# The last scans, the last three y and the first tile's index are reordered in a state-space and expert kernel

## What is computed

```python
x = L0_attn_u                              # (16, 512, 256)
xn = layernorm(x)
# state-space part
Bu = einsum('bld,nd->bln', u, B_w)         # u = xn
h[t] = sigmoid(log_lambda) * h[t-1] + Bu[t]    # written in the reference as an FFT convolution
y = einsum('bln,dn->bld', h, C_w) + D * u
# expert part
aff = (xn @ waff.T) / (|xn| * |waff| + 1e-9)
cap = clip(floor(S * sigmoid(aff.mean() - threshold)), 4, S)
mask = one_hot(argmax(softmax(aff))) * (rank of aff within its sequence and expert < cap)
out = sum over experts e of gelu((xn * mask_e) @ W1[e] + b1[e]) @ W2[e] + b2[e]
result = x + y + out
```

## Time and profile before

| | us |
|---|---|
| median of 3 runs (633.16 to 633.51) | 633.2 |
| the profiled execution, its own time | 634.01 |
| its span, first to last instruction | 632.1 |
| outside the span | 1.9 |
| PE busy | 580.8 (92%) |
| DVE, ACT, POOL busy | 431.0, 432.6, 460.8 |
| mean granted TensorE clock | 0.957 |

### The profile page before, as it was taken

How to read it: one execution, slowest core, us unless ns; L and a number is a source line. 1 busy time by engine, 2 the same in 40 slices (tenths; PEclk the granted TensorE clock), 3 DMA queues, 4 the chain that set the end, 5 groups by cost and what they waited for, 6 DMA issues and landing times.

```text
span 632.1 us, 16452 instructions
## 1 busy us (share of the span) xinstructions
PE 580.8 (92%) x4597; PEld 492.8 (78%) x4598; DVE 431.0 (68%) x831; ACT 432.6 (68%) x783; POOL 460.8 (73%) x618
## 2 busy tenths in 40 slices
PE   2987868989889999999999999999999999999992
PEld 1555545657678998989898898989898898989882
DVE  5789998987988989885655555645555555646554
ACT  4877677845978977886766767575766667575750
POOL 1999887971055434888878788888888888888855
PEclk9979778879799999999999999999999999999997
DMA  8993865736321314512222212122212212111110
GB/s 310 412 391 138 267 221 182 239 157 228 111 91 40 101 35 121 182 53 69 70 80 77 77 54 58 52 72 73 68 45 59 75 45 66 57 58 34 52 45 31
DMA packets 33588, 72.63 MB, mean 115 GB/s; under 512 B 6520, under 2 KB 19089, under 8 KB 33553
## 3 DMA queue, kind: packets, MB, share of 16 engines
q1 hardware_dynamic: 21488, 46.67, 20.9%
q0 software_dynamic: 11232, 25.20, 13.1%
q10 hardware_dynamic: 832, 0.31, 0.2%
HBM read 50.64 MB, written 27.00 MB: 123 GB/s over the span
## 4 chain that ended last, share of the span: by engine, by line
PE 75%; DVE 10%; issue 6%; ACT 5%; DMA 2%; POOL 1%; DVEq 0%; ACTq 0%; SPq 0%; POOLq 0%
PE ps_bu L919 10%; PE ps_bu L920 10%; PE ps_bu L921 10%; PE ps_t L890 5%; PE ps_t L892 5%; PE ps_t L891 5%; PE ps_y L892 5%; PE ps_y L890 5%; PE ps_y L891 5%; PE ps_bu L744 3%; ACT area L560 2%; PE ps_t L726 2%; PE ps_y L758 2%; PE ps_num L872 1%; PE ps_t L801 1%
## 5 line engine op out<-in xcount | busy, mean ns | idle before, releaser
L1364 DVE SCALAR_TENSOR_TENSOR ring<-ring,h_scale 128x512 f16<-128x512 f32 x156 | 115.9, 751 | 138.3 <-ACT ring L686 137.5
L919 PE MATMUL ps_bu<-area,ring 128*128 x616 | 167.9, 273 | 0.3 <-issue 0.3
L920 PE MATMUL ps_bu<-area,ring 128*128 x616 | 167.9, 273 | 0.0
L921 PE MATMUL ps_bu<-area,ring 128*128 x616 | 167.9, 273 | 0.0
L686 ACT ACTIVATE ring<-ring,h_act 128x512 f16<-128x512 f32 x144 | 104.0, 722 | 27.1 <-ACT ring L678 27.1
L494 POOL DMA_INDIRECT out<-ring,idx_b x74 | 94.7, 1280 | 17.3 <-issue 12.4
L456 POOL DMA_INDIRECT work<-xn_rows,idx_x x70 | 86.9, 1241 | 24.8 <-issue 24.2
L678 ACT ACTIVATE ring<-ps_t,b1t,inv_in 128x256 f32<-128x256 f32 x156 | 78.6, 556 | 33.2 <-PE ps_t L892 27.9
L504 POOL DMA_INDIRECT work<-base_rows,idx_b x74 | 79.2, 1070 | 17.1 <-issue 15.7
L890 PE MATMUL ps_t<-work,area 128*128 128x256 f16 x312 | 85.1, 273 | 1.7 <-ACT work L588 1.7
L892 PE MATMUL ps_t<-work,area 128*128 128x256 f16 x312 | 85.0, 273 | 0.0
(11 more groups left out here) (289 smaller groups left out, 1074.3 us busy)
## 6 DMA issues: line engine op xcount, KB each, us to landing
ring<-L_ffn_W SPq DMA_DIRECT2D x14, 1024.0 KB, 6.4
xn_rows<-area SPq DMA_DIRECT2D x8, 1024.0 KB, 8.6
base_rows<-area SPq DMA_DIRECT2D x8, 1024.0 KB, 7.2
area<-L_attn_u SPq DMA_DIRECT2D x7, 1024.0 KB, 19.1
work<-L_ffn_W SPq DMA_DIRECT2D x3, 1024.0 KB, 5.8
area<-L_ffn_W SPq DMA_DIRECT2D x3, 1024.0 KB, 5.4
work<-base_rows,idx_b POOLq DMA_INDIRECT x74, 2.8
out<-ring,idx_b POOLq DMA_INDIRECT x74
```

Source lines behind the costliest of these rows:

```text
L919: t.matmul(dst, hh, wh, start=(c == 0), stop=False)
L920: t.matmul(dst, hh, wl, start=False, stop=False)
L921: last = t.matmul(dst, hl, wh, start=False, stop=(c == C - 1))
L1364: v.scalar_tensor_tensor(out=hlo[p][:, cs], in0=h32[:, cs], scalar=h_scale[:, bass.ds(e, 1)], in1=hhi[p][:, cs], op0=ALU.mult, op1=ALU.sub ...
```

## The change

PE forms y of b = 14 before it transposes the last router sums, and y of b = 15 right after the affinity sum, ahead of most of the zero rows. In DVE's loop the denominators move behind `states(15)`. The adds of y for b = 13, 14 and 15 leave DVE: ACT copies `ps_y` to a buffer (`copy_y`), and POOL adds it (`add_y` on POOL, two adds of 128x512 each). The buffers are parts of `g_bc` and `work`, so `base_store(7)` now stands ahead of `raw_in(13)` and `raw_in(14)` in SP's list. ACT's `weight_sum(12)`, which stood ahead of the search, goes into its first half after round n = 5. The places in the second half move from n = 4, 5, 7, 10 to 1, 3, 5, 8. The index is formed in two steps: first the two columns of tile 0 (`idx_ok` 1), then the rest (`idx_ok` 2); POOL gathers tile 0 after the first.

```diff
@@ SP
             base_store(5)
             xn_store(7)
+            base_store(6)
             raw_in(12)
-            base_store(6)
+            base_store(7)
             raw_in(13)
             raw_in(14)
-            base_store(7)
             raw_in(15)
@@ POOL, after the 16 products
+            def add_y(b):
+                pool.wait_ge(s["y_out"], b - MOVED + 1)
+                for q in range(2):
+                    x = slice(q * 2 * D, (q + 1) * 2 * D)
+                    last = g.tensor_tensor(xu_(b)[:, x], y_out[b][:, x], xu_(b)[:, x], ALU.add)
+                last.then_inc(s["base_ok"], 1)
+            pool.wait_ge(s["dx_ok"], 2 * B)
+            add_y(B - 3)
+            add_y(B - 2)
             pool.wait_ge(s["sig_ok"], 1)
...
             g.tensor_scalar(cap, cap, 4.0, float(S), ALU.max, ALU.min).then_inc(s["cap_ok"], 1)
+            add_y(B - 1)
@@ POOL, gathers
+            bound = pool.to_reg(TOKENS - 1)
             pool.wait_ge(s["idx_ok"], 1)
-            bound = pool.to_reg(TOKENS - 1)
...
             for m in range(5):
+                if m == 1:
+                    pool.wait_ge(s["idx_ok"], 2)
                 gates = rows_in(m, m % 4, gates)
@@ ACT
+            def copy_y(b):
+                act.wait_ge(s["y_ok"], b + 1)
+                if b == B - 1:
+                    act.wait_ge(s["base_ok"], B - 2)
+                a.copy(y_out[b], ps_y[:, :]).then_inc(s["y_out"], 1)
...
+                if b == B - 1:
+                    copy_y(B - 3)
+                    a.activation(small[:, 62:63], lam_c, ACT.Exp)
+                    copy_y(B - 2)
                 if b in HIGHS:
                     high_part(HIGHS.index(b), raw_at(HIGHS.index(b)))
...
-            a.activation(small[:, 62:63], lam_c, ACT.Exp)
...
             a.activation(small[:, 62:63], lam_c, ACT.Gelu)
-            act.wait_ge(s["dx_ok"], 2 * B)
-            weight_sum(EARLY, junk_late)
+            copy_y(B - 1)
...
+            def first_half(n):
+                if n == 5:
+                    act.wait_ge(s["dx_ok"], 2 * B)
+                    weight_sum(EARLY, junk_late)
             def second_half(n):
-                if n == 4:
+                if n == 1:
                     split_x(0, 0)
                    zero_rows(0)
                    zero_rows(1)
-                if n == 5:
+                if n == 3:
                     step(0, 0)
                    zero_rows(2)
                    zero_rows(3)
-                if n == 7:
+                if n == 5:
                     step(1, 1)
-                if n == 10:
+                if n == 8:
                     step(2, 0)
...
-            find(key_hi, 14, s["hi_found"], None)
+            find(key_hi, 14, s["hi_found"], first_half)
@@ PE
-                wait(pe, s["base_ok"], b)
+                if b <= MOVED:
+                    wait(pe, s["base_ok"], b)
+                else:
+                    pe.wait_ge(s["y_out"], b - MOVED)
...
-            zero_row(0)
-            zero_row(1)
+            states_out(B - 2)
             routed(B - 1)
+            zero_row(0, range(0, 2))
             pe.wait_ge(s["aff_ok"], 1)
...
-            states_out(B - 2)
-            zero_row(2)
+            states_out(B - 1)
+            zero_row(0, range(2, C))
+            zero_row(1)
...
-            states_out(B - 1)
+            zero_row(2)
             zero_row(3)
             zero_row(4)
...
-            pe.wait_ge(s["idx_ok"], 1)
+            pe.wait_ge(s["idx_ok"], 2)
@@ DVE
-                if b > 1:
+                if b > 1 and b - 2 < MOVED:
                     add_y(b - 2)
...
                 if b == 14:
                     norms()
+                if b == 15:
                     denominators()
...
-            add_y(B - 2)          # behind L1193
...
-            add_y(B - 1)          # behind L1226
...
+            def index(j0, j1):    # L1263 to L1270 on columns j0 to j1
+            index(0, 2)
+            index(2, NS)
```

More of the change, by code:

```diff
@@ L172, in moe_ssm_kernel @@
         junk_late = part(work, 3 * QD, UW // 2).bitcast(F16)
+        y_out = {B - 3: part(g_bc, UW // 2, QD), B - 2: part(work, 0, QD), B - 1: part(g_bc, UW // 2, QD)}
+        MOVED = B - 3
         raw_late = part(work, 4 * QD + E * D, UW)
@@ L226, in moe_ssm_kernel @@
             "w_in0", "w_in1", "w_in2", "w_in3", "w_late0", "w_late1",
-            "ve_ok", "std", "rstd_ok", "xn_ok", "xt_ok", "xt_out", "bu_ok", "scan_ok", "num_ok", "y_ok", "dx_ok", "base_ok",
+            "ve_ok", "std", "rstd_ok", "xn_ok", "xt_ok", "xt_out", "bu_ok", "scan_ok", "num_ok", "y_ok", "dx_ok", "base_ok", "y_out",
             "xn_out0", "xn_out1", "xn_out2", "xn_out3", "xn_out4", "xn_out5", "xn_out6", "xn_out7",
@@ L790, in _, with zero_row @@
                     bound(n, ps_g[:, 0:P]).then_inc(s["bound_ok"], 1)
-            def zero_row(e):
+            def zero_row(e, chunks=range(C)):
                 n = E + e
@@ L799, in zero_row @@
                     pe.wait_ge(s["counts_used"], 1)
-                for c in range(C):
+                for c in chunks:
                     last = t.matmul(zero_out(e // 2)[:, e % 2 * D:(e % 2 + 1) * D],
@@ L803, in zero_row @@
                                     raw_at(n)[:, c * D:(c + 1) * D], start=(c == 0), stop=(c == C - 1))
-                last.then_inc(s["g_pe"], 1)
-            zero_row(0)
-            zero_row(1)
+                if C - 1 in chunks:
+                    last.then_inc(s["g_pe"], 1)
+            states_out(B - 2)
             routed(B - 1)
+            zero_row(0, range(0, 2))
             pe.wait_ge(s["aff_ok"], 1)
@@ L1262, in _, with cols @@
             iv, none = mask_slot, part(work, 2 * TE, NS)
-            link(v.scalar_tensor_tensor(out=gj(found_in), in0=gj(group_out), scalar=0.5,
-                                        in1=first.rearrange("p (g a) -> p g a", a=1).to_broadcast([P, 4, NS]),
-                                        op0=ALU.is_ge, op1=ALU.mult))
-            link(v.tensor_tensor(found_in, group_out, found_in, ALU.add))
-            link(v.tensor_reduce(iv, found_in.rearrange("p (g j) -> p j g", j=NS), AX.X, ALU.add))
-            link(v.tensor_scalar(none, iv, 0.5, float(4 * TOKENS), ALU.is_lt, ALU.mult))
-            link(v.scalar_tensor_tensor(out=iv, in0=iv, scalar=-1.0, in1=none, op0=ALU.add, op1=ALU.add))
-            v.tensor_copy(idx_all, iv).then_inc(s["idx_ok"], 1)
+            def index(j0, j1):
+                def cols(x):
+                    return x.rearrange("p (g j) -> p g j", j=NS)[:, :, j0:j1]
+                link(v.scalar_tensor_tensor(out=cols(found_in), in0=cols(group_out), scalar=0.5,
+                                            in1=first.rearrange("p (g a) -> p g a", a=1).to_broadcast([P, 4, j1 - j0]),
+                                            op0=ALU.is_ge, op1=ALU.mult))
+                link(v.tensor_tensor(cols(found_in), cols(group_out), cols(found_in), ALU.add))
+                link(v.tensor_reduce(iv[:, j0:j1], found_in.rearrange("p (g j) -> p j g", j=NS)[:, j0:j1, :], AX.X, ALU.add))
+                link(v.tensor_scalar(none[:, j0:j1], iv[:, j0:j1], 0.5, float(4 * TOKENS), ALU.is_lt, ALU.mult))
+                link(v.scalar_tensor_tensor(out=iv[:, j0:j1], in0=iv[:, j0:j1], scalar=-1.0, in1=none[:, j0:j1],
+                                            op0=ALU.add, op1=ALU.add))
+                v.tensor_copy(idx_all[:, j0:j1], iv[:, j0:j1]).then_inc(s["idx_ok"], 1)
+            index(0, 2)
+            index(2, NS)
             tc = tcmp.rearrange("p (j e) -> p j e", e=E)
@@ L1315, in kept_mask @@
                 dve.wait_ge(s["kept_inv"], 1)
-                dve.wait_ge(s["idx_ok"], 1)
+                dve.wait_ge(s["idx_ok"], 2)
                 v.tensor_scalar(mask_slot, ps_num[:, 0:NS], 0.5, None, ALU.is_ge).then_inc(s["mask_ok"], 1)
```

## The result

The changed kernel took 635.91 us, median of nine runs (633.91 to 637.75), beside 633.16 us for the kernel before on the same chip (632.20 to 634.28). The ratio is 1.0041, with a 95% interval of 1.0025 to 1.0057: slower by more than the 0.2% that a measurement of this kernel can tell. The time lay within the forecast's range, but its class was the second in the forecast's order (slower 0.37, no change 0.39). In a second set of runs the unchanged kernel after came out at 1.0064 (1.0037 to 1.0090).

A forecast was written before the change was run, and what follows sets the result against it. PE's tile stage was taken as a fixed block, so up(0)'s start and new gaps set the total. -0.8 (gather) + 1.4 (tile 1) + 0.2 (clock) = +0.8 on 633.2: 634.0 us, range 630.8 to 636.8.

The forecast's parts named there:

- the forecast's own part of it: Central case for the total: no change, 634.0 us, range 632.6 to 635.3; chance 0.44.
- the late unit 12: Rival: raw_in(12) lands after ACT wants it in the search, at 165.2; 634.0 to 638.2 us, typically 636.5; chance 0.16.
- the late product: Rival: PE's y of 14 and transposes keep the product at 150.5, search 3 us later; 637.0 us; chance 0.06.
- Two of the signs that the prediction named: hi_found later than before, at about 179; a PE gap of about 1.4 us ahead of up(1), released by DVE's x_low.
- Affinities: Scan ahead of the denominators, DVE's add gone: affinity product done at 147.6 for 150.55, a gain of 3.0 us.
- The keys: DVE's key chain loses 2.1 us beside two POOL adds (bounds 0 and 2.5); key_hi_ok at 156.2, 0.9 us earlier.
- The search: weight_sum(12) adds 2.0 us to the first half: hi_found 179.2, low keys 181.6, first gather 0.8 us earlier.
- From the index to `up(0)`: Between the split of tile 0 and up(0) nothing changes; the gather's 0.8 us gain enters the sum.
- this wait as a possibility: PE's counts for the index 2 us later if PE stays at half clock; idx_ok 1 at 180.4, not 177.7.
- Tile 1: Ahead of up(1): an extra search round delays hidden(0) and x_low(1), so PE waits 1.4 us (bounds 0.1 and 1.5).
- Clock: PE's idle ahead of up(0) may slow part of it: 0.2 us beyond the 1.4 us gap, bounds 0 and 1.5.
- Later places at 0: Search's second half after up(1): ACT, put 3 us back, makes it up where hidden(4) waited; cost 0.

The follow-up runs named there:

- the last set: Final runs, on another chip where the kernel before took 649.5 us: cuts to DVE's list, ACT's search or both with scales late, and index in one step with scales late.
- PE kept busy: Kernel after with 28 matmuls of unused result between PE's turn of tile 0 and up(0); 635.13 us, 1.0035.
- index in one step: Kernel after with the index formed in one step, as before the change; 633.48 us, 1.0016.
- scales late: Kernel after with the tile scales moved behind the low part of tile 0 in DVE's list, index still in two steps; 633.46 us, 1.0015.
- after, again: Kernel after, unchanged, run again for its spread and a second profile; 636.44 us, 1.0064.
- sum of one column: Kernel after with weight_sum(12) inside the search reading one column of 2048; 634.60 us, 1.0024.
- places back: Kernel after with the steps of the search's second half back at n = 4, 5, 7, 10; 635.45 us, 1.0026.
- scales late, places 1 2 4 7: Kernel after with the tile scales behind the low part of tile 0 and the steps at n = 1, 2, 4, 7; 633.86 us, 1.0012.
- short search: Kernel with scales late, rounds 12 and 13 of the search's second half left out, on another chip; 649.83 us, 1.0014.

## Why the forecast was right in its range and wrong in its reasons

The time lay in the range, 0.6 us above the forecast's own part of it (632.6 to 635.3), and the difference was +2.75 us for +0.8. That the range held it is partly luck: its upper end was drawn for the late unit 12 and the late product, and neither came. Two of the signs that the prediction named did not come either: `hi_found` was at 177.5 and not near 179, and neither profile of the kernel after has a gap ahead of `up(1)`.

**Affinities: right in the profile, too large for the median.** The product was forecast at 147.6. The eight profiles with the new first stage ahead of the last set lie between 145.96 and 148.44, mean 147.4. But the only other profile with the old first stage has it at 149.19, not 150.55, and the profiled execution of before was 0.85 us slower than its median. The gain of 3.0 us was taken from one execution that ended late; against the median it is nearer to 2.2.

**The keys: right in kind, too dear.** The two adds of POOL meet DVE's key operations:

```profile
153.20 1.37 DVE L1226 CAST work<-work 128x512 f32<-128x512 int32 x1
154.49 2.12 DVE L1227 TENSOR_TENSOR work<-small,work 128x512 f32<-128x512 f32 x1
...
152.88 2.80 POOL L421 TENSOR_TENSOR area<-work,area 128x512 f32<-128x512 f32 x2 [1.67 <-ACT work L613]
```

The cast of the keys took 1.37 us for 0.43, and the next operation 2.12 for about 1.0. Only the first lies ahead of `key_hi_ok`, so 0.9 us and not 2.1 fell on the search; the other 1.1 fell on DVE's list, which had no room. From the product to `key_hi_ok` it took 7.95 us (forecast 8.6).

**The search: right.** `weight_sum(12)` took 1.91 us in it, and the fourteen rounds with the low keys 25.3 us, forecast 25.4. POOL's gate was at 180.00 right behind the low keys, without idle (forecast 181.8; most of the difference is the earlier product and the cheaper keys). But it was a near tie: `idx_ok` 1 came at 179.93 and the low keys at 179.90. In the second profile of the same kernel the index was last:

```profile
180.66 0.19 POOL L401 TENSOR_TENSOR small<-ones 128x1 f32<-128x1 f32 x1 [0.51 <-DVE work L1311]
```

Unit 12 was issued at 156.65 and never waited for: that rival fell.

**From the index to `up(0)`: this step failed.** The prediction followed DVE only up to `idx_ok` and said "From the split of tile 0 to `up(0)` nothing changes". I had counted the two-step index as time off `idx_ok` and not as six more operations on DVE (0.16 to 0.37 us each, and one of them 1.15 us where it met POOL's low keys). In the earlier trace rows the copies of L588 stand one line ahead of `up(0)`, and I did not ask what they wait for. It is `largest(14)`, which in the kernel before ended at 188.03, only 1.3 us ahead of the copies at 189.32: a gather 3.3 us earlier had to run into it. The turn-to-`up(0)` time rose from 2.32 to 4.03 us.

The two-step index is only about a third of it. Behind the product `largest(14)` ended at 37.5 us before and at 41.2 after (41.6 in the second profile), although two adds of y, 2.45 us, had left the list. Some 6 us are new: 2.2 for the index in two steps, 2.0 for the two key operations beside POOL, 0.5 for ACT's sum, and a wait for PE's counts that was not there before, 1.25 us in the first profile and 1.86 in the second:

```profile
160.11 0.17 DVE L1239 COPY end<-ps_bu 128x8 f32<-128x8 f32 x1 [1.25 <-PE ps_bu L869]
```

The prediction had this wait as a possibility, 2 us on `idx_ok` if PE stayed at half clock, and left it out of everything behind. That the forecast of `up(0)` still fits (42.0 us behind the product, measured 42.2 and 42.6) is luck: two errors cancel, a cheaper key chain and an unseen list.

**Tile 1: right in kind, two thirds of its size.** The gap ahead of `up(1)`, released by `x_low`, is 0.81 to 0.94 us in the three kernels with the changed places where the clock stays up, for 1.4 forecast; in the kernel after the slow clock covers it. ACT's 1.26 us of issue took up 0.3 of the extra round (0.95 are left).

**Clock: the right place, the wrong price.** 0.2 us beyond the gap was the value taken, with bounds of 0 and 1.5. Tile 1 and clock together were to make `up(0)` to `up(1)` 7.72 us; the two profiles have 7.79 and 8.74, mean 8.27. The idle was forecast "up to 5 us", and a stretch of slow clock of 3.4 or 6.9 us was not priced as likely.

**Later places at 0: this failed too, in hiding.** The forecast said that ACT would make up three us where `hidden(4)` had waited, and that moves after `up(1)` cost nothing while PE is the bound. ACT's search ends 3.1 us later than before, at 225.11 for 222.02. Not the rounds make it late but the waits between them: 5.8 us in the kernel after (2.64 for the rows, 1.73 for `largest(14)`, 0.95, 0.29 and 0.17 in the gelus) for 1.4 before, since two rounds in place of five now hide the gather. DVE is late as well: kept begins 79.8 us behind the product for 75.8 before. Where PE is late itself, `down(4)` stays on its floor and this costs nothing; where PE comes early, the gate takes 0.3 to 0.9 us of it back. Which of the two holds it differs. With PE kept busy, the index in one step and the scales late, kept comes 1.9 to 2.2 us behind the search without idle of DVE ahead, so DVE's list is the later; only in the last row of the table does DVE wait 0.48 us for ACT. This gate is a part of why repairing the first cause gave equality and no gain.

**The sum.** Take from each profile the time from the product to `down(4)`, subtract the 99.33 us of before, 3.1 us for the mean product (150.55 to 147.4), and add the 0.85 us by which before's profile exceeds its median. Beside what was measured against the median of before:

| kernel | product to `down(4)` | worked out | measured |
|---|---|---|---|
| after | 103.36 | +1.8 | +2.75 |
| after, again | 104.70 | +3.1 | +3.66 |
| PE kept busy | 103.72 | +2.1 | +2.35 |
| index in one step | 102.32 | +0.7 | +0.70 |
| scales late | 101.88 | +0.3 | +0.68 |
| sum of one column | 103.09 | +1.5 | +1.69 |
| places back | 104.76 | +3.2 | +2.54 |
| scales late, places 1 2 4 7 | 101.65 | +0.1 | +0.95 |

All eight agree within 1 us, so no cost of more than about 1 us outside this stretch is needed to explain the loss. Of the forecast's shortfall, about 1.9 us against the median, 0.85 is the product's gain, 0.55 the clock and 0.4 `up(0)`, the last two from two profiles. Not settled is why before gains 0.85 us in its other executions; only one profile of it was read, and that these 0.85 us lie ahead of the product is assumed.

## What to carry to other kernels

When a wait is shortened, read what stands behind the waiting engine in its list and what that waits for: here a zero-row copy on ACT, released by the end of DVE's list, was due only 1.3 us after that list's end, so of 3.3 us gained by the gather 1.7 were lost there. Splitting an operation in two so that its first half comes early lengthens the list of the engine that does it, and every waiter further down that list pays. And when steps are put earlier among fillers, as the rounds of the search here, count the idle that they open: the fillers were hiding a latency.

## What was not expected of the hardware

**A slow clock makes the loss vary.** With the same 3.3 to 3.4 us of idle ahead of `up(0)`, the clock was at 0.50 for 3.4 us in one execution and for 6.9 in another, 0.95 us apart from `up(0)` to `up(1)`. The Trainium skill, "TensorE: Matmul & The Clock Gate", says in Part 1, on the clock gate, that the monitor runs free and that the same kernel therefore sees different numbers of slow matmuls; the two profiles agree.

**The same idle, another clock.** With the scales late, PE idled 1.66 us ahead of `up(0)` on the first chip and the clock stayed at 1.00; on the other chip, with 1.66 and 1.67 us of idle, the first 16 to 17 matmuls of tile 0 ran at half clock. No run here shows why.

**A two-column operation can cost 1.15 us.** The last operation of the first index step is a cast of 128x2 elements. It took 1.15 us beside POOL's add of 128x512 (1.26 us from 178.64), and 0.17 us in the second profile of the same kernel, where the two did not meet. "A small operation" is a statement about its own work, not about what it may have to wait out.

**On the other chip the tile stage had idles that the first never showed**: up to 3.2 us ahead of ACT's gelus, with a releaser that the trace calls remote, 8.9 us in six of them in the profile with the short search. One of them lies inside the search in each of the four profiles. What they are stays open.
